# Edge-attribute gathers split between the sort and the ends of layers 1 and 2, and gate biases written to PSUM by ScalarE, in a four-layer graph network on one Trainium2 core

## The chip, the core and the metric

The kernel runs on one NeuronCore of a Trainium2 chip. The core has five instruction streams that run side by side: TensorE (PE, matmuls into the accumulator memory PSUM), VectorE (DVE), ScalarE (ACT), GpSimd (POOL) and SyncE (SP, which here only starts transfers). They wait for each other through semaphores. The metric is the device time of one execution in microseconds; lower is better.

## The reference

Four graph layers over 12,500 nodes (64 features) and 200,000 edges. After each one the nodes become `x = layernorm(x + layer(x))`. Cut to what matters:

```python
# layer 0: attention by destination, edge attributes of 2 columns, moments of z = x W_fc^T
a   = z[src] @ wa0 + z[dst] @ wa3 + e2_term + constant
out = segment_sum(softmax_by_dst(leaky(a))[:, None] * (z[src] + ez), dst)
# layer 1: plain sum
out = segment_sum(x[src], dst)
# layer 2: attention by source, edge attributes of 16 columns, then a gated update
h   = relu(concat(x[src], edge_attr_16, x[dst]) @ W_att1.T + b_att1)
alpha = softmax_by_src(h @ W_att2.T + b_att2)
msg = segment_sum(alpha[:, None] * (x[dst] @ W_lin.T + b_lin), src)
gi, gh = x @ W_ih.T + b_ih, msg @ W_hh.T + b_hh
r, z = sigmoid(gi_r + gh_r), sigmoid(gi_z + gh_z)
n   = tanh(gi_n + r * gh_n)
out = where(degree > 0, (1 - z) * n + z * msg, x)
# layer 3: attention by destination
out = segment_sum(softmax_by_dst(leaky(concat(x[src], x[dst]) @ W.T + b)) * x[src], dst)
```

(This text counts layers from 0, as the code does. The "ends of layers 1 and 2" of the short description are the ends of the first two, layers 0 and 1 here.)

## The kernel before

The program is a row of blocks. At the end of a block all five engines meet; the next block starts when the last of them is through.

**Block 1** sorts the edges by source. **Block 2** sorts them by destination (DVE, ACT and PE: a bitonic sort of 262,144 keys in 171 stages) and, beside that, brings the 16 attribute columns of each edge (with a one and the destination, 18 words, the array `rec16`) into source order. That is the work of `take_gpsimd`. The 200,704 places of an edge list are laid out as 128 partitions of W = 1568 columns, and one gather on POOL (`indirect_dma_start`) fetches one column, 128 rows of 72 bytes. `ESTEPS` = 196 steps of `G16` = 8 gathers fill a ring of 8 slots, `e_rows`; SP stores four steps at a time to `rec_s`. The steps are paced. While the sort runs, DVE also makes one-hot tables for a histogram, 200 steps, of which the first `BEGUN` = 24 are done in block 1. Step s of the gathers waits for histogram step `24 + s * 176 // ESTEPS` (line 733 makes it, the wait is in front of the gather of line 606). At three quarters of the steps POOL also sends 98 scatters (`scatter_seeds`, line 574).

**Blocks 3 to 6** are the four layers, made by `edge_layer`. In each POOL gathers 1568 columns of the node table (line 1202), and DVE and ACT form running sums along the sorted edges, which SP stores to `sums`. At the end of a layer comes a chain: the last sums are stored; POOL waits for that and gathers `ends` (line 1211); PE, DVE and ACT join the partial sums of the 128 partitions; SP stores `special` (line 1254); POOL waits for that and gathers the sums of the 98 node blocks, `got` (line 1218, 98 gathers). Seven groups of 14 node blocks are normed by DVE and ACT as they arrive (`normed_nodes`), and SP stores each to the next table (line 1755). At the end of layer 1 POOL, after `got`, scatters the new nodes (line 574, 98 scatters). Layer 2 then reads `rec_s`.

**The gated update** (`gated_nodes`) is the node stage of layer 2. Its 98 node blocks are cut into 28 parts, in each group of 14 three parts of four blocks and one of two. Each engine goes through a fixed order. At its step t, PE does `turn(t)` and `project(t-1)`. ACT does `own(t)`, `bend(t-3)`, `sigmoid_half(t-2)`, `keep(t-1)` and, where a part closes a group, `square`, `root` and `copy_rows`. DVE does `mix(t)`, `update(t-3)`, `candidate(t-2)` and, for closing parts, `center`, `variance` and `finish`. For one part: `turn` transposes (line 2044), `keep` copies that out of PSUM (line 1994), `project` adds the biases by three matmuls with a row of ones (line 2054, `bias4`) and then the products with `w_all` (line 2058), `sigmoid_half` (line 2002) reads the sums, `candidate`, `bend` and `update` (last line 1941) finish the part. `project(b)` may overwrite PSUM once `update(b-2)` is done (`new`). After `finish`, POOL scatters 14 columns of seeds for layer 3.

## Time and profile before

| | us |
|---|---|
| median of 3 runs | 11759.01 (11755.06 to 11760.62) |
| the profiled execution | 11769.89 |
| its span, first to last instruction | 11768.2 |
| busy: POOL | 8350.4 (71%) |
| busy: DVE | 5629.5 (48%) |
| busy: ACT | 2619.6 (22%) |
| busy: PE | 2530.8 (22%) |

The profile is of one execution. "Busy" is the time in which an engine worked on an instruction; time in which it waited, or in which its sequencer prepared the next one, is not counted. In the timeline a row gives the start, the duration, the engine, the line of the kernel, the operation and the tiles (written <- read), and in brackets how long the engine had been idle before and what ended that. "issue" means that it waited for nothing that is recorded. PEclk is the granted TensorE clock as a share of 2.4 GHz; its two levels are 0.5 and 1.0, and a stretch shows a mean of them.

### The profile page before, as it was taken

The numbers are of one execution on the slowest core, as the hardware profiler recorded it, in microseconds if no ns is written. First come the engines' busy times: TensorE is split into PE (matmuls) and PEld (weight loads), VectorE is DVE, ScalarE is ACT, GpSimd is POOL, SyncE is SP. The second block draws the span as 40 slices with busy tenths as digits, with TensorE's granted clock in tenths as the row PEclk, the third lists the DMA queues.
The fourth block names the chain that finished last, engine by engine and source line by source line (L and its number), as shares of the span: only waits on it lengthen the run. The fifth ranks groups of instructions, "written<-read, shape, count | busy, mean of one in ns | idle before, by whom it ended". The sixth has DMA issues, their size and how long they took to land. (4 is left out here: it accounts for less than half of the span.)

```text
span 11768.2 us, 56949 instructions
## 1 busy us (share of the span) xinstructions
PE 2530.8 (22%) x12070; PEld 2016.1 (17%) x12070; DVE 5629.5 (48%) x13769; ACT 2619.6 (22%) x3769; POOL 8350.4 (71%) x8546
## 2 busy tenths in 40 slices
PE   2322434320200000000000001666666640000000
PEld 2211323220200000000000000555555530000000
DVE  9999898970422222421111112677777542222223
ACT  1155555540111111112222220111111121111111
POOL 0077777777777777667777777777777657777776
PEclk8555555555555555555555555787888755555555
DMA  7000000011222222211111111333333212222222
GB/s 223 11 14 13 13 14 14 7 28 32 58 55 55 55 54 55 52 52 53 53 51 53 53 52 46 86 87 86 86 88 87 59 27 55 53 55 55 55 54 49
DMA packets 689050, 631.35 MB, mean 54 GB/s; under 512 B 453662, under 2 KB 511671, under 8 KB 687681
## 3 DMA queue, kind: packets, MB, share of 16 engines
q0 software_dynamic: 273056, 240.52, 10.7%
q1 hardware_dynamic: 414782, 380.90, 10.0%
q10 hardware_dynamic: 864, 6.29, 0.1%
q14 instruction: 252, 2.06, 0.1%
q8 instruction: 96, 1.57, 0.1%
HBM read 322.26 MB, written 304.83 MB: 53 GB/s over the span
## 5 line engine op out<-in xcount | busy, mean ns | idle before, releaser
L1202 POOL DMA_INDIRECT l_rows<-table,l_sources x4704 | 4477.1, 952 | 1474.8 <-issue 1433.4
L606 POOL DMA_INDIRECT e_rows<-in_rec,base x1568 | 1668.6, 1064 | 1059.8 <-DVE marks L733 579.0
L1202 POOL DMA_INDIRECT l_pair<-table,l_slab x1568 | 1505.1, 960 | 483.5 <-issue 459.6
L1401 DVE TENSOR_TENSOR_SCAN l_totals<-l_factor,banks 128x510 f32<-128x510 f32 (+3 forms) x672 | 752.8, 1162 | 1677.1 <-ACT banks L1556 1675.9
L1566 ACT COPY l_kept<-l_totals 128x476 f32<-128x476 f32 (+3 forms) x672 | 639.2, 967 | 3191.5 <-DVE l_totals L1401 3181.9
L1332 DVE TENSOR_TENSOR l_score<-l_rows,base 128x14 f32<-128x14 f32 x224 | 41.3, 185 | 2672.0 <-DMA l_rows<-table,l_sources 2672.0
L1518 PE MATMUL banks<-ident,l_kept 128*65 128x128 f32 (+2 forms) x4 | 1.9, 463 | 5865.0 <-DVE junk L1450 5865.0
L1518 PEld LDWEIGHTS banks<-ident,l_kept 128*65 128x65 f32 (+2 forms) x4 | 0.7, 170 | 5866.8 <-DVE junk L1450 5866.8
L751 PE MATMUL banks<-marks 125*128 125x98 bf16 x3200 | 623.3, 366 | 1235.3 <-DVE marks L733 1235.3
L388 DVE COPY_PREDICATED area<-banks,area 128x2048 f32<-128x2048 int32 x342 | 869.0, 2596 | 0.2
L751 PEld LDWEIGHTS banks<-marks 125*128 125x128 bf16 x3200 | 460.3, 148 | 1386.2 <-DVE marks L733 1282.0
L1508 PE MATMUL banks<-w_each,l_turned 128*128 128x288 f32 (+1 forms) x1344 | 658.7, 579 | 166.9 <-ACT l_turned L1588 166.9
L465 ACT COPY area<-area 128x2048 f32<-128x2048 f32 x342 | 642.8, 1930 | 0.2
L1320 DVE SCALAR_TENSOR_TENSOR l_junk<-banks,w_out 128x144 f32<-128x144 f32 x1568 | 407.9, 303 | 472.6 <-PE banks L1512 470.7
L1512 PEld LDWEIGHTS banks<-w_in,l_turned 128*128 128x128 f32 x3136 | 599.1, 235 | 190.0 <-issue 123.7
L1588 ACT COPY l_turned<-banks 128x512 f32<-128x512 f32 x448 | 248.1, 588 | 1673.1 <-PE banks L1497 1672.7
L1512 PE MATMUL banks<-w_in,l_turned 128*128 128x144 f32 x3136 | 606.8, 332 | 0.0
L1556 ACT COPY banks<-l_rows 128x476 f32<-128x476 f32 x224 | 196.0, 907 | 1504.4 <-DMA l_rows<-table,l_sources 1504.4
L462 ACT COPY area<-area 128x2048 f32<-128x2048 f32 x164 | 311.5, 1899 | 863.9 <-DVE area L388 800.9
L1425 DVE SCALAR_TENSOR_TENSOR l_kept<-l_kept,l_factor,l_message 128x65 f32<-128x65 f32 x1568 | 452.9, 289 | 81.2 <-DVE l_pair L1311 2.9
L382 DVE COPY_PREDICATED area<-banks,area 128x1024 f32<-128x1024 int32 x328 | 451.8, 1438 | 36.5 <-ACT area L462 32.4
L1497 PE MATMUL banks<-ident,l_pair 128*128 128x128 f32 x1568 | 270.8, 324 | 735.9 <-DMA l_pair<-table,l_slab 735.0
(310 smaller groups left out, 6302.7 us busy)
## 6 DMA issues: line engine op xcount, KB each, us to landing
l_rows<-table,l_sources POOLq DMA_INDIRECT x4704
sums<-l_kept SPq DMA_DIRECT2D x112, 476.0 KB
sums<-l_kept SPq DMA_DIRECT2D x224, 231.0 KB
sums<-l_kept SPq DMA_DIRECT2D x112, 462.0 KB
seeds<-zeros SPq DMA_DIRECT2D x130, 392.0 KB
sums<-l_kept SPq DMA_DIRECT2D x112, 448.0 KB
l_pair<-seeds SPq DMA_DIRECT2D x224, 224.0 KB, 3.3
e_rows<-in_rec,base POOLq DMA_INDIRECT x1568
```

The lines of the kernel that those rows point to most:

```text
L382: V.copy_predicated(key_to[:, :, i, :], swap.rearrange("p (x l) -> p x l", l=low), key_was[:, :, 1 - i, :])
L388: ins_ = V.copy_predicated(to[i], m, was[1 - i])
L465: AC.copy(to[i], was[i]).then_inc(s["copied"], 1)
L606: GP.indirect_dma_start(e_rows[:, u, g, :], None, A["rec16"], bass.IndirectOffsetOnAxis(e_ids[:, s * G16 + g:s * G16 + g + 1], 0)).then_in ...
L751: mm = PE.matmul(ps["ds".index(k)][:, 0:NB], hot[0][0:EP, i % HOTS, :, c], hot[1][0:EP, i % HOTS, 0:NB, c], start=s == 0 and c == 0, stop= ...
L1202: GP.indirect_dma_start(pair[:, u, g, 0:D] if gated else rows[:, u, g, :], None, table[l], bass.IndirectOffsetOnAxis(at, 0)).then_inc(rows ...
L1320: V.scalar_tensor_tensor(junk[:, g % 2, :], hidden_at(g), 0.0, extra["w_out"][:], ALU.max, ALU.mult, accum_out=score[:, u, g:g + 1]).then_ ...
L1401: V.tensor_tensor_scan(flat(totals[:, s % 2, h, 0:n, :]), flat(factor[:, s % 2, 0:n, :]), flat(fresh[s % 2][h][:, 0:n, :]), 0.0, ALU.mult, ...
L1425: V.scalar_tensor_tensor(kept[:, u, g, 0:M], old, factor[:, u, g:g + 1], message[:, u, g, :], ALU.mult, ALU.add).then_inc(kp.sem, 1)
L1508: PE.matmul(ps[4 + i][:, 0:n * H1], turned[:, u % 2, G * P:], extra["w_edge"][:, a:a + n, :].rearrange("p g h -> p (g h)"), start=True, st ...
L1512: mm = PE.matmul(hidden_at(g), turned[:, u % 2, g * P:(g + 1) * P], extra["w_in"][:], start=False, stop=True, skip_group_check=True)
L1566: AC.copy(kept[:, s % KR, :, a:a + n], totals[:, s % 2, h, 0:n, 1:G + 1].rearrange("p f g -> p g f")).then_inc(S["kept"].sem, 1)
```

## The change

It has two parts.

**Gathers.** `take_gpsimd` now stops 64 columns short: `ESTEPS` is (1568 - 64) / 8 = 188. The last 64 columns of attributes are fetched by POOL into a tile of their own, `late_rows`, in four pieces (`LATE_AT`): 22 behind the last node gather of layer 0 and ahead of the gather of `ends`, 14 at the very end of layer 0, 16 and 12 at the same two places of layer 1. SP fetches their ids in block 2 and stores `late_rows` to `rec_s` at the end of layer 1 (`save_late`). The tile of zeros of block 1 now lies in `late_rows`.

**Biases.** The three bias matmuls of `project` are gone. A tile `bias_all` holds the biases on all partitions (one matmul with ones and one copy at the start of layer 1, in place of three copies to `bias4`), and ACT copies it into the PSUM banks ahead of `keep`, in three copies (`set_bias`). `project(b)` waits for `biased(b)` in place of `new(b-2)`, and `set_bias(b)` waits for `new(b-2)`.

```diff
         G16 = 8
-        ESTEPS = W // G16
+        LATE_AT = ((0, 22), (22, 14), (36, 16), (52, 12))
+        LATE = sum(n for _, n in LATE_AT)
+        ESTEPS = (W - LATE) // G16
+        def take_late(pool, part):
+            a, n = LATE_AT[part]
+            pool.wait_ge(late_ids_in, 16)
+            for c in range(a, a + n):
+                GP.indirect_dma_start(late_rows[:, c, :], None, A["rec16"],
+                                      bass.IndirectOffsetOnAxis(late_ids[:, c:c + 1], 0)).then_inc(late_in, 16)
+        def save_late(sp):
+            sp.wait_ge(late_in, 16 * LATE)
+            sp.dma_start(rec_s.rearrange("(p c) w -> p c w", p=P)[:, W - LATE:, :], late_rows[:]).then_inc(late_saved, 16)
+            sp.wait_ge(late_saved, 16)
...
                     in_turn(STEPS, RING, [(0, one)])
+                    first_do.get("gpsimd_tail", nothing)(pool)
                     for u in range(KR):
                         pool.wait_ge(*saved[u].done(saves(u)))
...
                     then_do.get("gpsimd", nothing)(pool)
+                    first_do.get("gpsimd_end", nothing)(pool)
...
                     then_do.get("sync", nothing)(sp)
+                    first_do.get("sync_end", nothing)(sp)
...
             pe.wait_ge(w2_loaded, 16 * N_W2)
             PE.matmul(ps[6][:, 0:3 * D], w_lin[:], w_hh_t[:], start=True, stop=True)
             PE.matmul(ps[6][0:1, 3 * D:6 * D], b_col[:], w_hh_t[:], start=True, stop=True).then_inc(w2_mixed, 1)
+            pe.wait_ge(bias_made, 1)
+            PE.matmul(ps[7][:, 0:5 * D], ones[0:1, :], bias[:], start=True, stop=True).then_inc(bias_spread, 1)
...
+                    def set_bias(b, *_):
+                        g, v, a, n, o, u = of(b)
+                        if b >= 2:
+                            act.wait_ge(*new.done(b - 2))
+                        else:
+                            act.wait_ge(tail["kept"], 3)
+                        for to, at, w in sums_of(u):
+                            ins = AC.copy(to[:, 0:n, :], bias_all[:, None, at:at + w].to_broadcast([P, n, w]))
+                        ins.then_inc(biased.sem, 1)
...
-                    in_turn(N, 2, [(0, own), (3, bend), (2, sigmoid_half), (1, keep), (4, square), (5, root),
+                    in_turn(N, 2, [(0, own), (3, bend), (2, sigmoid_half), (1, set_bias), (1, keep), (4, square), (5, root),
                                    (6, copy_rows)])
...
                         pe.wait_ge(*kept.done(b))
-                        if b >= 2:
-                            pe.wait_ge(*new.done(b - 2))
-                        ways = ((both[u], 0, 2 * D), (hidden_in[u], 2 * D, 2 * D), (message_in[u], 4 * D, D))
-                        for to, at, w in ways:
-                            PE.matmul(to[:, 0:n, :].rearrange("p j f -> p (j f)"), ones[0:1, :],
-                                      bias4[:, J * at:J * at + n * w], start=True, stop=False, skip_group_check=True)
+                        pe.wait_ge(*biased.done(b))
                         for j in range(n):
-                            for to, at, w in ways:
+                            for to, at, w in sums_of(u):
```

How POOL's queue runs from block 2 to the end of layer 1, first before, then after the change (an `UNCONDITIONAL_BRANCH` is the edge of a block; lines 574 and 576 are the scatters, 606 and 625 the gathers of attributes, 1202 and 1223 those of nodes):

```order
L606 DMA e_rows<-in_rec,base 128x18 x392
L1053 UNCONDITIONAL_BRANCH
...
L1202 DMA l_rows<-table,l_sources 128x66 x1540
L1211 DMA l_ends<-sums,first_end_d 128x68
L1218 DMA got<-sums,end_at_d 128x68 x98
L1602 UNCONDITIONAL_BRANCH
...
L1202 DMA l_rows<-table,l_sources 128x64 x1568
L1211 DMA l_ends<-sums,first_end_d 128x64
L1218 DMA got<-sums,end_at_d 128x64 x98
L574 DMA seeds<-X,seed_at_s 213248x64 x98
```

```order
L625 DMA e_rows<-in_rec,base 128x18 x376
L1074 UNCONDITIONAL_BRANCH
...
L1223 DMA l_rows<-table,l_sources 128x66 x1540
L590 DMA late_rows<-in_rec,late_ids 128x18 x22
L1233 DMA l_ends<-sums,first_end_d 128x68
L1240 DMA got<-sums,end_at_d 128x68 x98
L590 DMA late_rows<-in_rec,late_ids 128x18 x14
...
L1223 DMA l_rows<-table,l_sources 128x64 x1568
L590 DMA late_rows<-in_rec,late_ids 128x18 x16
L1233 DMA l_ends<-sums,first_end_d 128x64
L1240 DMA got<-sums,end_at_d 128x64 x98
L576 DMA seeds<-X,seed_at_s 213248x64 x98
L590 DMA late_rows<-in_rec,late_ids 128x18 x12
```

The gathers of attributes ahead of the block's edge are 376 where they were 392 (and 1128 where they were 1176 ahead of the scatters), and four runs of late gathers stand on POOL at the ends of the two layers, two of them ahead of `ends`.

ACT in the gated update, around the second part of a group, before and after (line 1994, after it 2025, is `keep`; 2002, after it 2043, is `sigmoid_half`; 2034 is `set_bias`):

```order
L2007 ACTIVATE l_pair<-l_pair 128x128 [waits gru_reset]
L2002 ACTIVATE l_pair<-banks 128x512 [waits gru_new,gru_made]
L1994 COPY l_pair<-banks 128x512 [waits gru_made,gru_turned]
L1987 COPY l_pair<-X 128x2x64 [waits gru_turned]
L2007 ACTIVATE l_pair<-l_pair 128x256 [waits gru_reset]
```

```order
L2048 ACTIVATE l_pair<-l_pair 128x128 [waits gru_reset]
L2043 ACTIVATE l_pair<-banks 128x512 [waits gru_new,gru_made]
L2034 COPY banks<-bias_all 128x512 [waits gru_new]
L2034 COPY banks<-bias_all 128x512
L2034 COPY banks<-bias_all 128x256
L2025 COPY l_pair<-banks 128x512 [waits gru_made,gru_turned]
L2018 COPY l_pair<-X 128x2x64 [waits gru_turned]
L2048 ACTIVATE l_pair<-l_pair 128x256 [waits gru_reset]
```

`keep` now stands behind three copies, and behind their wait for `new`.

PE at the same place, before and after (2044 and 2085 are `turn`, 2058 and 2094 the products with `w_all`):

```order
L2044 MATMUL banks<-ident,l_pair 128x128 x3
L2054 MATMUL banks<-bias,ones 128x512 [waits gru_new,gru_kept]
L2054 MATMUL banks<-bias,ones 128x512
L2054 MATMUL banks<-bias,ones 128x256
L2058 MATMUL banks<-w_all,l_pair 128x128 x2
L2058 MATMUL banks<-w_all,l_pair 128x64
```

```order
L2085 MATMUL banks<-ident,l_pair 128x128 x3
L2094 MATMUL banks<-w_all,l_pair 128x128 [waits gru_biased,gru_kept]
L2094 MATMUL banks<-w_all,l_pair 128x128
L2094 MATMUL banks<-w_all,l_pair 128x64
L2094 MATMUL banks<-w_all,l_pair 128x128 x2
```

The three bias matmuls are gone from between `turn` and the products.

## Rows read from the trace of the kernel before

**Rows 1.** The page, part 1: busy time (share) and instructions of each engine.

```profile
PE 2530.8 (22%) x12070; PEld 2016.1 (17%) x12070; DVE 5629.5 (48%) x13769; ACT 2619.6 (22%) x3769; POOL 8350.4 (71%) x8546
```

**Rows 2.** Stretches of block 2: busy (instructions) of each engine, PEclk, DMA share, GB/s.

```profile
2600.00:2700.00 100.00, 0.00 (x0) 0.00 (x0) 0.00 (x0) 0.00 (x0) 75.66 (x80) 0.50 0.11 18
```

**Rows 3.** Stretches, line 606 alone: length, POOL busy (number of gathers), PEclk, DMA share, GB/s.

```profile
560.00:1201.00 641.00, 475.58 (x448) 0.50 0.09 13
...
2590.00:2880.00 290.00, 216.57 (x229) 0.50 0.13 26
```

**Rows 4.** Timeline: start, duration, engine, line, tiles, idle before; a paced gather; block 2's end.

```profile
1201.30 1.19 POOL L606 DMA_INDIRECT e_rows<-in_rec,base  x1 [2.25 <-DVE marks L733]
...
2875.26 0.95 POOL L606 DMA_INDIRECT e_rows<-in_rec,base  x1 [0.30 <-issue]
2884.35 0.32 SPq L1225 DMA_DIRECT2D l_sources<-dsrc  x1
```

**Rows 5.** Timeline, end of layer 0: POOL, DVE's last, SP's first of the next block.

```profile
4878.90 0.95 POOL L1202 DMA_INDIRECT l_rows<-table,l_sources  x1 [0.30 <-issue]
4895.77 0.97 POOL L1211 DMA_INDIRECT l_ends<-sums,first_end_d  x1 [15.93 <-DMA sums<-l_kept]
4905.26 0.95 POOL L1218 DMA_INDIRECT got<-sums,end_at_d  x1 [8.53 <-issue]
...
5026.61 0.94 POOL L1218 DMA_INDIRECT got<-sums,end_at_d  x1 [0.30 <-issue]
...
5042.98 1.09 DVE L1700 TENSOR_TENSOR X<-banks,l_var_n 128x896 f32<-128x896 f32 x1
5047.96 0.33 SPq L1225 DMA_DIRECT2D l_sources<-dsrc  x1
```

**Rows 6.** Timeline, end of layer 1: POOL, and the first instruction of layer 2's block.

```profile
7012.38 0.94 POOL L1202 DMA_INDIRECT l_rows<-table,l_sources  x1 [0.30 <-issue]
...
7023.34 0.94 POOL L1211 DMA_INDIRECT l_ends<-sums,first_end_d  x1 [10.02 <-DMA sums<-l_kept]
...
7280.45 0.97 POOL L574 DMA_INDIRECT seeds<-X,seed_at_s  x1 [0.30 <-issue]
7290.88 0.29 ACT L1581 COPY l_runs_on<-marks 128x7 f32<-128x7 f32 x2 [126.81 <-PEq L1602]
```

**Rows 7.** Groups of the gated update (9308 to 9635): busy, mean ns, idle before.

```profile
L2054 PE MATMUL banks<-bias,ones 1*128 1x512 f32 (+1 forms) x168 | 80.6, 624 | 14.4 <-ACT l_pair L1994 13.1 <-DVE l_pair L1941 1.1
```

**Rows 8.** Timeline of the gated update: a part of two blocks, and parts 12 and 13.

```profile
9391.94 1.35 PE L2054 MATMUL banks<-bias,ones 1*128 1x256 f32 x6 [0.51 <-ACT l_pair L1994]
...
9439.65 0.42 DVE L1941 SCALAR_TENSOR_TENSOR l_pair<-l_pair 128x256 f32<-128x256 f32 x1
...
9440.22 4.60 PE L2054 MATMUL banks<-bias,ones 1*128 1x512 f32 x6 [0.21 <-DVE l_pair L1941]
...
9444.75 5.38 PE L2058 MATMUL banks<-w_all,l_pair 128*128 128x128 f32 x24
...
9450.17 0.60 ACT L2002 ACTIVATE l_pair<-banks 128x512 f32<-128x512 f32 x1 [9.23 <-PE banks L2058]
9450.66 0.58 ACT L1994 COPY l_pair<-banks 128x512 f32<-128x512 f32 x1
...
9451.29 2.41 PE L2054 MATMUL banks<-bias,ones 1*128 1x512 f32 x6 [0.31 <-ACT l_pair L1994]
...
9453.64 4.47 PE L2058 MATMUL banks<-w_all,l_pair 128*128 128x128 f32 x24
```

**Rows 9.** Groups of layer 1, two kinds of ACT copy: busy, mean ns, idle before.

```profile
L1556 ACT COPY banks<-l_rows 128x476 f32<-128x476 f32 x112 | 107.3, 958 | 1504.4 <-DMA l_rows<-table,l_sources 1504.4
...
L1549 ACT COPY l_factor<-marks 128x476 f32<-128x476 f32 x112 | 65.6, 586 | 26.6 <-DVE junk L1268 26.6
```

**Rows 10.** Stretches of the gated update: busy (instructions) of each engine, PEclk, DMA share, GB/s.

```profile
9395.00:9434.00 39.00, 31.22 (x122) 23.57 (x122) 21.33 (x42) 11.24 (x23) 29.86 (x31) 0.65 0.22 38
...
9545.00:9606.00 61.00, 32.70 (x118) 24.86 (x118) 39.30 (x66) 15.97 (x28) 27.50 (x27) 0.57 0.09 16
```

More of the change, by code:

```diff
@@ L176, in build @@
         padded = sem("padded")
+        late_ids = sbt(top, "late_ids", [P, 64], I32)
+        late_rows = sbt(top, "late_rows", [P, 64, RE])
+        zeros = late_rows[:].rearrange("p c w -> p (c w)")[:, 0:W // 2]
         layer0 = ExitStack()
@@ L612, in take_sync @@
         def take_sync(sp):
-            sp.dma_start(e_ids, sid[0:NQ].rearrange("(p c) -> p c", p=P)).then_inc(e_ids_in, 16)
+            ids = sid[0:NQ].rearrange("(p c) -> p c", p=P)
+            sp.dma_start(e_ids, ids).then_inc(e_ids_in, 16)
+            sp.dma_start(late_ids[:], ids[:, W - LATE:]).then_inc(late_ids_in, 16)
             to = rec_s.rearrange("(p c) w -> p c w", p=P)
@@ L1804, in build @@
         bias = sbt(gated_ctx, "bias", [1, 5 * D])
-        bias4 = sbt(gated_ctx, "bias4", [1, 4 * 5 * D])
+        bias_all = sbt(gated_ctx, "bias_all", [P, 5 * D])
         w3 = sbt(gated_ctx, "w3", [P, 2, D])
@@ L1809, in build @@
         w2_made = Chain(sem("w2_made"))
+        bias_made, bias_spread = sem("bias_made"), sem("bias_spread")
         N_W2 = 29
@@ L1849, in gated_weights_vector @@
             link(V.tensor_copy(bias[:, 3 * D:4 * D], b_row[:, 2 * D:3 * D]))
-            link(V.tensor_copy(bias[:, 4 * D:], b_row[:, 6 * D:]))
-            for a, n in ((0, 2 * D), (2 * D, 2 * D), (4 * D, D)):
-                link(V.tensor_copy(bias4[:, 4 * a:4 * (a + n)].rearrange("p (j f) -> p j f", j=4),
-                                   bias[:, None, a:a + n].to_broadcast([1, 4, n])))
+            V.tensor_copy(bias[:, 4 * D:], b_row[:, 6 * D:]).then_inc(bias_made, 1)
+            dve.wait_ge(bias_spread, 1)
+            link(V.tensor_copy(bias_all[:], ps[7][:, 0:5 * D]))
         layer_ctx = ExitStack()
@@ L1887, in stage @@
                 of_group = lambda n: again(f"gru_{n}", 1, len(groups))
-                mixed, owned, turned, kept, made, gated, reset, tanh, new = (
-                    of_part(n) for n in ("mixed", "owned", "turned", "kept", "made", "gated", "reset", "tanh", "new"))
+                mixed, owned, turned, kept, made, gated, reset, tanh, new, biased = (
+                    of_part(n) for n in ("mixed", "owned", "turned", "kept", "made", "gated", "reset", "tanh", "new",
+                                         "biased"))
+                sums_of = lambda u: ((both[u], 0, 2 * D), (hidden_in[u], 2 * D, 2 * D), (message_in[u], 4 * D, D))
                 centered, squared, spread, rooted, x_done, near_done, copied = (
```

13 lines of the change are left out of this document (8 added, 5 removed).

## The prediction

> **What bounds the kernel now.** I read the page first: POOL is busy 71% of the span, no other engine over half [rows 1]. Since the blocks follow each other, each place that the change touches has its own last engine, so I read the timeline at four places.
>
> *Block 2.* From 2600 on PE, DVE and ACT do nothing, and POOL gathers attributes alone, 80 in 100 us [rows 2]. In the last stretch 229 gathers take from 2590 to 2876.2, which is 1.25 us each (0.95 busy, 0.30 between) [rows 3, 4]. The next block begins 8.1 us after the last gather's end. POOL ends this block by far, so a gather less is 1.25 us less, unless it is paced.
>
> *Ends of layers 0 and 1.* In layer 0 POOL is idle for 15.9 us between its last node gather and `ends`, and 8.5 us more until `got`; after its last `got` (end 5027.6) DVE still works to 5044.1, and the next block starts at 5048.0 [rows 5]. In layer 1 the first pause is 10.0 us. But its last engine is POOL: the last scatter ends at 7281.4, and the next block starts 9.5 us later [rows 6]. The reader should see that three of the four places are pauses with a length, and the fourth is none.
>
> *The gated update.* The bias matmuls take 80.6 us in all [rows 7], and they follow `keep` and precede the products, on the chain by which one part ends: `sigmoid_half`, `keep` of the next part, biases, products, `sigmoid_half` again [rows 8]. What POOL does there (98 scatters) ends last, but its last 14 wait for DVE's last group, so the chain sets the end.
>
> **The change, part by part.** The sum is made against the profiled execution (11769.9 us, of which 11768.2 is the span). It is 10.9 us above the median of the runs; I take that off at the end.
>
> *Block 2: -60.* Without pacing 64 gathers x 1.25 would be 80 us. But the first steps are paced by DVE. The last wait of some length is at 1201.30, after 448 gathers, at step 56 [rows 3, 4]; it asks for histogram step 24 + 56*176//196 = 74. After the change each step asks for a later one: histogram step 74 is asked for by step 54 (54*176//188 = 50). The table comes at the same time, so at 1201 POOL has 54 steps behind it and not 56. Left are 188 - 54 = 134 steps where 140 were. DVE's part of the block is untouched, so the 6 steps are missing at the end, where POOL is alone: 6 x 8 x 1.25 = 60 us. Past 1201 no pacing is near: 1120 gathers in 1675 us include 98 scatters, some 11 us a step, and the histogram needs less. Bounds: 50 (POOL loses another step to the pacing) and 80 (none at all).
>
> *22 gathers ahead of `ends` in layer 0: +11.9.* The 23rd slot after the gather at 4878.90 starts at 4878.90 + 23 x 1.25 = 4907.7, where `ends` now starts at 4895.8 [rows 5]. All that comes after `ends` shifts with it, the second pause too, which is a wait for the chain that `ends` starts. Of 27.5 us of gathers 15.6 are covered.
>
> *14 at the end of layer 0: +6.6.* The last one would end at 5027.55 + 17.5 = 5045.1. The block does not end there: at the end of layer 1 9.5 us lie between POOL's last transfer and the next block [rows 6], in block 2 8.1 [rows 4]. With 9.5 the next block starts at 5054.6, not at 5048.0 [rows 5]. With 8.1 it is 5.2.
>
> *16 in layer 1's tail: +10.3.* 7012.38 + 17 x 1.25 = 7033.6 against 7023.3 [rows 6].
>
> *12 at the end of layer 1: +15.0.* POOL is last there, so all 12 are paid. SP's store of `late_rows` starts when the last has landed and lies inside the same 9.5 us; if it takes longer than they last, up to 3 us come on top.
>
> So 36 of the 80 us are covered, 43.8 are paid, and the gathers give -60.0 + 43.8 = **-16.2**.
>
> *The gated update: -27.* The three copies are priced by two rows. An ACT copy of 476 columns between SBUF tiles, with a repeated operand, takes 0.586 us; one that writes PSUM, with a strided read, 0.958 [rows 9]. `sigmoid_half` and `keep`, 512 columns each, start 0.49 apart [rows 8]. By the first row three copies (512, 512, 256 columns) are 1.4 us for a part of four blocks and 0.9 for one of two; by the second 2.4. I take 1.4: the read of `bias_all` runs along contiguous columns, as in the first row.
>
> The biases cost 4.6 or 2.41 us by the clock for four blocks, 1.35 for two [rows 8]. Step by step:
> - Part 0: `set_bias` is done before there is data. -4.6.
> - Part 4, same chain, low clock: 4.6 - 1.4 = 3.2.
> - 14 parts, second and third of each group. Out of 80.6 us seven first parts take 7 x 4.6 and seven short ones 10.8, so these have 37.6, 2.7 each: 37.6 - 14 x 1.4 = 18.0.
> - Parts 8 to 24, every fourth: before them DVE does `finish`, then `update(b-2)` (ends 9440.07), then the biases start (9440.22) [rows 8]. Now `set_bias` waits for that update and `keep` stands behind it: 1.4 + 0.6 in place of 4.6. The short part's `set_bias` also stands ahead of `root`, for which `finish` waits, 1.0. Each 1.6, five times 8.0.
> - Parts 3 and 27: 2.1 together. The other short parts are behind `finish`: 0.
>
> Sum 35.9. Against it stands the clock. The products take 5.38 us at the lower and 4.47 at the higher level [rows 8]. PE is busy 31.2 of 39 us with a mean clock of 0.65, and in the last stretch 32.7 of 61 with 0.57 [rows 10]. Without the biases PE is busy some 20 of 35, as in the second row, so I price all products at the lower level: eight parts with 0.9 more and three with 0.5, 8.7. That leaves **-27**. Bounds: -6 (copies at 2.4 us: 21 more) and -38. The Trainium skill (TensorE: Matmul & The Clock Gate, Part 1) says that the clock follows how busy PE has been of late, a rule that speaks against taking matmuls away; by it the stage gives 27, without it 36. The Trainium skill (ScalarE: Activation LUTs, ACT is a hardware spline evaluator) calls PSUM ScalarE's faster destination; the PSUM row of this trace is the slower of the two, but its read is strided too. By the page the destination adds nothing and 1.4 and 27 stand; by the row taken as it is they are 2.4 and 6.
>
> *At nothing:* the extra matmul and copy of `bias_all` at the start of layer 1 (about 1 us more on DVE, while the first rows are still on their way), and the load of the 64 ids.
>
> Sum: 11769.9 - 60.0 + 43.8 - 27 = 11726.7 for the profiled execution, less 10.9: **11716 us** against the median of 11759 (-0.37%).
>
> **The rivals.**
> *A. No change that can be measured.* ACT's copies cost as the PSUM row says, and the stage gives 6. With 16 of the gathers that is -22: 11737. For it: the one row that writes PSUM. Against it: its read pattern, also seen in slow copies.
> *B. The clock stays up.* PE's work shrinks, but so do its waits. The stage gives 36 to 38: 11706.
> *C. Pacing costs nothing* (POOL makes up its lost steps, since it has fewer to do while DVE disturbs it): -80 in block 2, 11696. Against it: 1201.30 is a wait for DVE.
> *D. Slower.* `keep` and with it every product stands behind `set_bias`. If the copies into PSUM are held while PE writes there, ACT becomes the chain. The stage breaks even at 1.4 + 27/21 = 2.7 us a part, the kernel at 1.4 + 43/21 = 3.4, and it is 0.2% slower from 1.4 + 66.5/21 = 4.6, where a copy takes three times the 0.586 row. At 5 us it is 11716 + 21 x 3.6 = 11792. Against it: nothing in the trace shows an ACT copy beyond 1.0 us at that size.
>
> **How the numbers follow.** Forecast 0.62, A 0.16, B 0.12, C 0.06, D 0.04. The likeliest gives 11716. The range reaches from 11699 (between B and C) to 11741 (A; with block 2 at its bound of 50 it would be 11747) and leaves out about 2 in 10. A measurement of this kernel can tell 0.2%, 23.5 us, from no change. Faster by more: forecast, B and C, 0.80; within: A, 0.16; slower: 0.04.
>
> **What would show it.** In the new profile: block 2's last attribute gather at about 2815; the step that waits for the histogram near 1201 with 432 gathers behind it; `ends` of layer 0 12 us later after the last node gather than before, with no wait for the saves; a gap of 8 to 9.5 us between POOL's last transfer and the start of layers 1 and 2; `set_bias` copies of 0.6, 0.6 and 0.35 us; products of 5.4 us at PEclk 0.5; and the stage from the first `keep` to the last scatter some 27 us shorter. Wrong would be: a new wait between ACT and DVE at each part, late gathers of more than 1.25 us each, or a block 2 shorter by 80.

## The result, and the profile after

The changed kernel takes **11700.35 us** (median of 5 runs, 11698.78 to 11708.72), the kernel before 11759.01 (5 runs beside them, 11753.46 to 11762.34). The ratio is 0.9954, with a 95% interval of 0.9942 to 0.9966: 58.7 us or 0.5% faster. The forecast was 11716 (11699 to 11741). Sign and range hold; the middle is 16 us too high, and nearly all of that is one term.

The profiled execution of the changed kernel took 11700.35 us, its own median, with a span of 11698.6. The one of before was 10.9 us above its median, so differences between the two profiles hold some 11 us that belong to neither part of the change.

Busy times first (part 1 of the page after; engine, busy us, share of the span, instructions). They answer to [rows 1]: POOL is as busy as before, PE is 96 us less busy, ACT 32 more.

```profile
PE 2434.3 (21%) x11904; PEld 1961.6 (17%) x11904; DVE 5630.7 (48%) x13767; ACT 2651.5 (23%) x3853; POOL 8344.7 (71%) x8546
```

The timeline after, POOL and SP at the places of [rows 4] (start, duration, engine, line, operation and tiles, idle time before and its releaser):

```profile
1200.98 1.68 POOL L625 DMA_INDIRECT e_rows<-in_rec,base  x1 [3.01 <-DVE marks L754]
...
2814.19 0.94 POOL L625 DMA_INDIRECT e_rows<-in_rec,base  x1 [0.30 <-issue]
...
2823.28 0.32 SPq L1248 DMA_DIRECT2D l_sources<-dsrc  x1
...
2827.97 0.94 POOL L1223 DMA_INDIRECT l_rows<-table,l_sources  x1 [12.84 <-DMA l_sources<-dsrc]
...
4814.40 0.94 POOL L1223 DMA_INDIRECT l_rows<-table,l_sources  x1 [0.30 <-issue]
4815.65 0.94 POOL L590 DMA_INDIRECT late_rows<-in_rec,late_ids  x1 [0.30 <-issue]
...
4843.16 0.94 POOL L1233 DMA_INDIRECT l_ends<-sums,first_end_d  x1 [0.30 <-issue]
4852.49 0.94 POOL L1240 DMA_INDIRECT got<-sums,end_at_d  x1 [8.39 <-DMA sums<-l_special]
...
4973.58 0.94 POOL L1240 DMA_INDIRECT got<-sums,end_at_d  x1 [0.30 <-issue]
4974.82 0.94 POOL L590 DMA_INDIRECT late_rows<-in_rec,late_ids  x1 [0.30 <-issue]
...
4991.05 0.94 POOL L590 DMA_INDIRECT late_rows<-in_rec,late_ids  x1 [0.30 <-issue]
...
5001.52 0.33 SPq L1248 DMA_DIRECT2D l_sources<-dsrc  x1
...
6962.15 0.95 POOL L1223 DMA_INDIRECT l_rows<-table,l_sources  x1 [0.30 <-issue]
6963.41 0.94 POOL L590 DMA_INDIRECT late_rows<-in_rec,late_ids  x1 [0.30 <-issue]
...
6983.38 0.94 POOL L1233 DMA_INDIRECT l_ends<-sums,first_end_d  x1 [0.30 <-issue]
...
7252.30 0.94 POOL L590 DMA_INDIRECT late_rows<-in_rec,late_ids  x1 [0.30 <-issue]
...
7254.81 0.33 SPq L595 DMA_DIRECT2D rec_s<-late_rows  x1
...
7263.24 0.94 POOL L1210 DMA_INDIRECT l_first<-table,node_s  x1 [10.00 <-POOLq L1626]
```

Read it against [rows 4 to 6]. The wait near 1201 us is still there, with 432 gathers behind it. The last attribute gather starts at 2814.19. `ends` of layer 0 follows the last late gather without a wait. SP's store of the late rows, issued at 7254.81, lies inside the gap that follows POOL's last transfer.

| term | before | after | change | forecast |
|---|---|---|---|---|
| first gather of layer 0 | 2888.93 | 2827.97 | -61.0 | -60.0 |
| layer 0, end of the last node gather to `ends` | 15.9 | 27.8 | +11.9 | +11.9 |
| layer 0, last `got` to the first gather of layer 1 | 25.1 | 31.7 | +6.6 | +6.6 |
| layer 1, end of the last node gather to `ends` | 10.0 | 20.3 | +10.3 | +10.3 |
| layer 1, last scatter to the next block | 10.5 | 25.0 | +14.6 | +15.0 |
| gated update, first `got` gather to the last scatter | 314.9 | 275.2 | **-39.8** | **-27** |
| sum | | | -57.4 | -43.2 |

The sum of -57.4 lies close to the 58.7 us between the medians. The two spans differ by 69.6 us. The 12.2 us that are left between them lie in the loops of the layers (3.5, 3.8 and 3.8 us shorter in layers 0, 1 and 3, 1.4 longer in layer 2) and in the `got` stage of layer 1 (2.7 shorter), which the change does not touch. The profile of before stood 10.9 us above its median, so that is about where its surplus would be; no second trace of either kernel on this machine shows it.

Now the stage that gave more. ACT and PE in one group of 14 blocks, after, in the timeline (for [rows 8]):

```profile
9392.94 5.38 PE L2094 MATMUL banks<-w_all,l_pair 128*128 128x128 f32 x24 [2.08 <-ACT l_pair L2025]
...
9400.83 2.89 PE L2094 MATMUL banks<-w_all,l_pair 128*128 128x128 f32 x24 [1.65 <-ACT l_pair L2025]
...
9424.58 1.41 ACT L2034 COPY banks<-bias_all 128x512 f32<-128x512 f32 x3 [5.70 <-DVE l_pair L1972]
9425.93 0.58 ACT L2025 COPY l_pair<-banks 128x512 f32<-128x512 f32 x1
...
9426.56 4.56 PE L2094 MATMUL banks<-w_all,l_pair 128*128 128x128 f32 x24 [2.08 <-ACT l_pair L2025]
...
9431.16 0.60 ACT L2043 ACTIVATE l_pair<-banks 128x512 f32<-128x512 f32 x1 [3.30 <-PE banks L2094]
9431.65 1.41 ACT L2034 COPY banks<-bias_all 128x512 f32<-128x512 f32 x3
```

The three copies of `set_bias` take 1.41 us for four blocks. `keep` and the products follow in the order that was forecast, and the new wait for `update` stands ahead of `set_bias` (5.70 us). But products of four blocks also take 2.89 us. The granted clock in three such products, and below it that of four groups, after (window, length, busy time and instructions of PE, PEld, DVE, ACT, POOL, PEclk, DMA share, GB/s):

```profile
9392.94:9398.32 5.38, 5.38 (x25) 5.38 (x26) 0.87 (x3) 1.30 (x3) 4.16 (x5) 0.50 0.81 113
9400.82:9403.71 2.89, 2.88 (x24) 2.75 (x24) 2.75 (x5) 0.47 (x2) 2.28 (x3) 1.00 0.15 26
9433.62:9438.07 4.45, 4.45 (x26) 4.43 (x26) 4.28 (x8) 0.46 (x2) 3.54 (x4) 0.63 0.02 0
...
9356.60:9488.50 131.90, 72.47 (x392) 67.15 (x392) 83.64 (x166) 62.88 (x132) 100.58 (x98) 0.69 0.19 26
```

And the same of before, for the two products that the forecast took as the two levels, and for four groups:

```profile
9444.75:9450.13 5.38, 5.38 (x26) 5.38 (x26) 0.00 (x0) 0.00 (x0) 4.16 (x5) 0.50 0.04 5
9453.64:9458.11 4.47, 4.47 (x27) 4.47 (x26) 3.96 (x8) 0.00 (x0) 3.34 (x4) 0.62 0.02 0
...
9399.90:9550.10 150.20, 120.50 (x488) 91.17 (x488) 83.96 (x165) 43.45 (x84) 85.86 (x85) 0.66 0.11 20
```

Products wholly at 1.2 GHz take 5.38 us, wholly at 2.4 GHz 2.89. The 4.47 us of before were a mixture (clock 0.62), not the higher level. Over four groups PE's share of work fell from 80% to 55%, and the clock did not fall with it (0.66 and 0.69). A group takes 33.0 us (a quarter of 131.9) after 37.6 (of 150.2).

### The profile page after: what moved, and what is told of

It is laid out like the page before. It is cut to its first block and busy times, and to the rows that moved or that the text cites. A ratio compares the mean times of both kernels' runs of the same rounds, so it can differ in the third digit from the quotient of the medians.

```text
span 11698.6 us, 56700 instructions
## 1 busy us (share of the span) xinstructions
PE 2434.3 (21%) x11904; PEld 1961.6 (17%) x11904; DVE 5630.7 (48%) x13767; ACT 2651.5 (23%) x3853; POOL 8344.7 (71%) x8546
## 5 line engine op out<-in xcount | busy, mean ns | idle before, releaser
L625 POOL DMA_INDIRECT e_rows<-in_rec,base x1504 | 1611.0, 1071 | 1056.1 <-DVE marks L754 605.1
L1356 DVE TENSOR_TENSOR l_score<-l_rows,base 128x14 f32<-128x14 f32 x224 | 43.4, 194 | 2662.8 <-DMA l_rows<-table,l_sources 2662.8
L1403 DVE TENSOR_TENSOR banks<-l_rows,banks 128x476 f32<-128x476 f32 x448 | 423.9, 990 | 5.9 <-ACT banks L1565 5.9
```

Of the source, the lines that this page charges most:

```text
L625: GP.indirect_dma_start(e_rows[:, u, g, :], None, A["rec16"], bass.IndirectOffsetOnAxis(e_ids[:, s * G16 + g:s * G16 + g + 1], 0)).then_in ...
L1403: V.tensor_tensor(fresh[s % 2][h][:, 0:n, 1:G + 1], rows[:, u, :, a:a + n].rearrange("p g f -> p f g"), w.to_broadcast([P, n, G]), ALU.mul ...
```

## The experiments

The experiments ran on three other chips than the comparison above. There the kernel before takes 13338 to 13379 us, not 11759. The median gather of nodes is as long as in the first traces (0.94 us), and so are the copies and matmuls; but the late gathers of `z_after` take 1.08 us, and the node gathers of layer 0 start 1.45 us apart on average (`z_before`) where it was 1.27. `x_gathers`, `x_biases`, `x_pace` and `x_warm` ran on one chip, `y_pace`, `y_full`, `x_nobias` and `x_tight` on the second, `z_before`, `z_after`, `x_nopace` and `x_cover` on the third. So each run is read against the kernel before that ran beside it, and against `z_before`. An experiment of these shows what a part does there; it does not measure again the sizes of the first comparison.

**1. The gathers alone** (`x_gathers`), the three bias matmuls and `bias4` put back:

```diff
-                        pe.wait_ge(*biased.done(b))
+                        if b >= 2:
+                            pe.wait_ge(*new.done(b - 2))
+                        for to, at, w in sums_of(u):
+                            PE.matmul(to[:, 0:n, :].rearrange("p j f -> p (j f)"), ones[0:1, :],
+                                      bias4[:, J * at:J * at + n * w], start=True, stop=False, skip_group_check=True)
```

> The gathers alone: the 64 late gathers as in the changed kernel, the biases by matmuls as before. If the two parts of the change don't touch each other, block 2 ends 60 us earlier, the four pieces add 11.9, 6.6, 10.3 and 15, and the kernel is 16 us faster than before (ratio 0.9986); the stage of the gated update stays at 315 us (first `got` gather to the last scatter). Rival: the loops of the layers, which were 3.5 to 3.8 us shorter in three of the four layers of the changed kernel's profile, are shorter because of the late gathers; then they are shorter here too, against this kernel's own time, and it gains some 28 us (0.9976).

Measured: 1.0035 (1.0015 to 1.0055), slower by 35 us of the medians, where -16 was expected.

**2. The biases alone** (`x_biases`), with `ESTEPS = W // G16` and no late gathers:

> The biases alone: `set_bias` on ScalarE as in the changed kernel, all 196 steps of attribute gathers in block 2. From the two traces the stage of the gated update should take 275 us, 40 less than before, and the kernel should be 40 us faster (0.9966). The forecast, which let the products fall to the lower clock, had 27 less (0.9977). If the 40 came partly from the gathers, the stage is longer than 275 here.

Measured: 0.9983 (0.9960 to 1.0006), the stage 401.9 us, with 417.5 in `x_gathers` and 410.8 in `z_before`. The direction holds, the size does not, on this machine. The 1568 node gathers of layer 0 take 2278 us in `x_gathers` and 2279 here, those of layer 1 2175 and 2169, so the late gathers don't make the loops shorter; that rival falls.

**3. Both kernels there** (`z_before`, one execution, and `z_after`), unchanged:

> The kernel before, unchanged, once with a profile. The experiments so far ran on machines on which the kernel before takes 13338 to 13379 us, not 11759, and their traces show POOL's gathers, DVE's copies and ACT's copies as long as ever, but stretches in which engines wait for nothing that is recorded. This run gives the trace to compare with. Expected: block 2 ends with DVE's sort, not with POOL's gathers; the gathers of layers 0, 1 and 3 start 1.38 us apart, not 1.25; the stage of the gated update takes 417 us, as in x_gathers, not 315.

> The changed kernel, unchanged, on such a machine. If its two parts add up there as measured alone (x_gathers +35 us, x_biases -16), it is 19 us slower than before (1.0014). On a machine as in the first comparison it is 0.9954. Rival: the parts help each other there too, and it is faster than before (below 0.998).

Measured: in `z_before` the node gathers start 1.45, 1.38 and 1.38 us apart on average in layers 0, 1 and 3, and the stage of the gated update takes 410.8 us. `z_after` takes 0.9994 (0.9971 to 1.0016). The ratios of the parts measured alone add up to 1.0018, just outside that interval; with the intervals of the two parts, some 0.002 each, this does not speak against their adding up. So the change that gains 0.5% in the first comparison gains nothing that can be measured here.

From trace to trace: the four pieces cost 15.6, 14.7, 12.7 and 19.1 us, together 62.1 where 43.4 were paid at first, because the late gathers start some 1.4 us apart, not 1.25, and the block's end lasts longer.

And the four places are not all: from the first gather of layer 0 to the first of layer 2 `z_after` takes 5002 us and `z_before` 4925, 77 more, as in `x_gathers` against `x_biases` (76). Of the 15 us beyond the four places some 6 lie in the loop of layer 1 and 6 in its `got`; why was not looked into.

The stage of the gated update gives 7.2 us, not 39.8, and `x_gathers`, with the same stage as `z_before`, took 6.7 longer in it than that kernel, so 7.2 is known to a few us only. Of the 128 us that the stage of `z_after` is longer than in the first comparison, 112 are two waits of ACT at its beginning (59.4 and 52.5) for the semaphore that PE sets behind the products.

Block 2 is ended by DVE's sort there. The first instruction behind the sort (line 686 before, 707 after), in the timelines of `z_before` and then of `z_after`:

```profile
3123.43 1.98 DVE L686 TENSOR_SCALAR area<-area 128x2048 int32<-128x2048 int32 x1
```

```profile
3045.00 1.98 DVE L707 TENSOR_SCALAR area<-area 128x2048 int32<-128x2048 int32 x1
```

POOL's last attribute gathers end at 3041.5 and 2969.4, so 82 and 76 us ahead of it. Of the sort's 78 us no more than a part is the change's: the five runs with its gathers and its pace have this instruction at 3103, 3078, 3049, 3045 and 3031.

**4. The pace** (`x_pace`, and the same kernel again on another machine as `y_pace`):

```diff
-                paced = BEGUN + s * (2 * HSTEPS - BEGUN) // ESTEPS
+                paced = BEGUN + s * (2 * HSTEPS - BEGUN) // (W // G16)
```

> The changed kernel with one number changed: the pace of the attribute gathers is worked out with 196 steps again, so step s waits for the same histogram step as in the kernel before. If the pacing cost two of the eight steps, POOL has 448 gathers behind it at the wait near 1201 us (432 in the changed kernel), and layer 0 begins 20 us earlier: block 2 is 80 us shorter than before, the kernel 20 us faster than the changed one (0.9937 of before). Rival: the missing steps were lost to something else (memory traffic or the sort beside it), the wait near 1201 is no limit, and the start of layer 0 moves by less than 5 us.

> The same kernel as x_pace: the changed kernel, with the pace of the attribute gathers worked out with 196 steps again. There the machine handed out instructions late on all engines (13338 us for the kernel before), DVE's sort ended block 2 at 3115 and the pace could not matter. If this run is on a machine on which the kernel before takes some 11760 us again, the expectation is the first one: 448 gathers behind POOL at the wait near 1201 us, layer 0 begins 20 us earlier than in the changed kernel (2808 in place of 2828), and the kernel takes 11680 (0.9933 of before). Rival: the start of layer 0 moves by less than 5 us, 11700.

Measured: 1.0044 (1.0022 to 1.0067) and 1.0065 (1.0040 to 1.0090). Where 20 us less were expected it is slower than the changed kernel (0.9994, on another chip), by more than the intervals. On one and the same chip `y_pace` stands clear of `y_full` (1.0013, up to 1.0028), which has the changed kernel's pace, while `x_pace` does not stand clear of `x_gathers` (1.0035) and `x_warm` (1.0013, up to 1.0037). The instruction behind the sort comes at 3104 and 3161 us, against 3031 to 3103 with the changed kernel's pace. Whether the two steps come back where POOL ends the block was not measured. But the pace does something that my forecast did not see, so I took it away altogether.

**5. No pace** (`x_nopace`), the two lines with the wait for the histogram taken out:

> The changed kernel with the wait for the histogram taken out of the attribute gathers, so POOL runs ahead of DVE's sort as fast as it can. With the pace loosened by 4% (x_pace, y_pace) the kernel was 1.0044 and 1.0065 of before, where kernels with the same gathers and the changed kernel's pace (x_warm, y_full) were 1.0013. If gathers that run early delay the sort, this is worse still: over 1.007. If the pace does not matter where the sort ends block 2, it is 1.001. On a machine as in the first comparison, where POOL ends block 2, it should gain the 43 us that POOL waits there: 0.992.

Measured: **1.0800** (1.0772 to 1.0829), over 1000 us slower. In `x_nopace` POOL gathers without a pause until 2091 us. Windows before and behind that point (columns as above):

```profile
600.00:2090.00 1490.00, 178.57 (x535) 76.15 (x536) 427.01 (x322) 236.73 (x129) 1158.10 (x1082) 0.50 0.11 14
2100.00:2600.00 500.00, 175.74 (x912) 138.46 (x912) 447.44 (x298) 244.78 (x160) 0.00 (x0) 0.53 0.00 0
```

What DVE waits for in the first of them, and then the DMA queues of it (packets, MB, share of 16 engines):

```profile
DVE marks L752 <- remote: 940.1, 30, 34.7
DVE marks L752 <- issue: 103.7, 3, 34.7
```

```profile
q0 software_dynamic: 34622, 10.04, 9.2%
q1 hardware_dynamic: 4896, 10.03, 1.7%
q8 instruction: 4, 0.07, 0.0%
q14 instruction: 12, 0.10, 0.0%
```

While POOL gathers DVE works 427 of 1490 us, and when POOL stops 447 of 500. "remote" is what the profile writes when it finds no instruction that ended a wait. The kernel says what line 752 waits for: it may overwrite a one-hot table once PE has counted an earlier one (`summed`, set behind the matmuls of line 770). The same wait in the first comparison is put down to PE:

```profile
DVE marks L754 <- PE banks L772: 6.4, 10, 0.7
```

So PE has to be looked at. Its matmuls of one histogram step, first in the first comparison, then in `x_nopace` around one of DVE's waits, and what PE waits for there between 600 and 2090 us:

```profile
1286.34 3.15 PE L772 MATMUL banks<-marks 125*128 125x98 bf16 x16 [12.79 <-DVE marks L754]
```

```profile
1123.14 0.14 PEld L770 LDWEIGHTS banks<-marks 125*128 125x128 bf16 x1 [2.65 <-issue]
1124.13 1.10 POOL L623 DMA_INDIRECT e_rows<-in_rec,base  x1 [0.30 <-issue]
1124.54 0.34 PE L770 MATMUL banks<-marks 125*128 125x98 bf16 x1 [2.46 <-issue]
1125.53 1.09 POOL L623 DMA_INDIRECT e_rows<-in_rec,base  x1 [0.30 <-issue]
1125.94 0.14 PEld L770 LDWEIGHTS banks<-marks 125*128 125x128 bf16 x1 [2.66 <-issue]
1125.95 1.23 DVE L752 TENSOR_TENSOR marks<-count_j,work 125x2048 bf16<-125x2048 bf16 x1 [34.69 <-remote]
```

```profile
PE banks L770 <- issue: 1294.9, 526, 3.2
```

In the first comparison 16 matmuls of a step take 3.15 us. Here PE gets out one instruction, a weight load or a matmul, every 1.40 us, and a step of 16 of each takes 44.8 us, which is the distance from one of DVE's long waits to the next. So DVE waits for PE, and PE waits for nothing recorded. PE is back at 16 matmuls in 3.15 us at 2122.84, some 30 us after POOL's last gather. `z_after` has such stretches too, but short ones (up to 1332 us, for one, with matmuls mostly 2.8 us apart).

The two queues named "instruction" move 16 packets in 1490 us; in the same window of `z_after`, where POOL pauses for the pace, they move 35, and DVE works 1185 us. That count alone decides nothing, since engines that get less done also need fewer instructions. The reading: PE's instructions come late while POOL gathers without a pause, so the pace is what keeps the sort going. The rows show that the two go together; that the gathers hold up PE's instructions, and by what way, is inferred and not shown. The expectation of `y_pace` spoke of late instructions on all engines; the rows here show them on PE. The Trainium skill (Runtime: NRT & Kernel Launch, Instruction fetch mechanics) says that each sequencer fetches through a DMA queue of its own and that the cost is mostly hidden. If fetching is what PE's waits are, it was not hidden on these machines; in the first comparison there are no such waits (41 packets in the same window, and DVE waits in it only for ACT and PE, 8.5 us at most).

**6. A tighter pace** (`x_tight`):

```diff
-                paced = BEGUN + s * (2 * HSTEPS - BEGUN) // ESTEPS
+                paced = min(2 * HSTEPS - 1, BEGUN + s * (2 * HSTEPS - BEGUN) // (ESTEPS - 8))
```

> The changed kernel with the pace of the attribute gathers tightened: the divisor is 180 in place of 188 (196 in x_pace). Theory, from x_nopace (while POOL gathers without a pause DVE works 28% of the time and 89% once it stops): the other engines get their instructions in POOL's pauses, so more pauses end the sort earlier. In the changed kernel's run on such a machine POOL's last attribute gather was at 2969 and DVE's sort ended at 3055, so there is room; divisor 196 cost 0.3% to 0.5%, so 180 should give about as much: the sort ends 40 to 60 us earlier, the kernel is at 0.995 to 0.997 of before. Rival: the pace matters only where it is taken away altogether, and x_pace was a chance; then 0.999 to 1.002. On a machine as in the first comparison, where the gathers end the block, the tighter pace costs one or two steps more, 10 to 20 us.

Measured: **0.9967** (0.9951 to 0.9982), the size that the theory gave. The instruction behind the sort, in `x_tight`'s timeline:

```profile
3001.89 1.98 DVE L707 TENSOR_SCALAR area<-area 128x2048 int32<-128x2048 int32 x1
```

It comes earlier than in each of the five runs with the changed kernel's pace, and in `x_nopace` it comes at 4052. It is the one version that is faster than before on these machines by more than its interval. Its interval ends below that of `y_full` on the same chip (0.9997 to 1.0028) but overlaps those of `z_after` and `x_nobias`, so that the tighter pace beats the changed kernel's is likely and not settled. Nor is it shown that it works by way of PE's late instructions.

**7. Fewer late columns** (`x_cover`):

```diff
-        LATE_AT = ((0, 22), (22, 14), (36, 16), (52, 12))
+        LATE_AT = ((0, 12), (12, 8), (20, 8), (28, 4))
```

> The changed kernel with 32 late columns in place of 64, in pieces that the pauses of the first comparison cover: 12 and 8 in layer 0, 8 and 4 in layer 1. On a machine as in the first comparison: three of the eight steps that 32 columns are (four, less one for the pace) leave block 2, -30 us, and some 7 us are paid (4 x 1.25 for the last piece, 1 or 2 for the rest); with the biases' -40 that is 11759 - 63 = 11696, the changed kernel's time within 5 us, with half the columns moved. Where block 2 ends with the sort, nothing is gained in it; half of the 61 us that the four pieces cost there (x_gathers against x_biases) are paid: between x_biases (0.9983) and the changed kernel (1.0014).

Measured: 0.9984 (0.9965 to 1.0003), not to be told from `z_after` beside it. But in the traces the pieces cost 2.2, 9.0, 2.5 and 6.6 us against `z_before`: 20.3 us for 32 columns where 64 cost 62.1. The pieces inside the pauses ahead of `ends` are nearly free at their own place, as the forecast priced them. From the first gather of layer 0 to the first of layer 2, though, `x_cover` takes 4956 us, 32 more than `z_before`, where 64 columns take 77 more; 5 of the 11 us beyond the four places lie in the `got` of layer 1.

**8. Work added on TensorE** (`x_warm`, `y_full`), one more matmul behind each part's products and four behind a group's last:

```diff
                         mm.then_inc(made.sem, 1)
+                        for _ in range(4 if b in closes else 1):
+                            PE.matmul(ps[6 + u][:, 0:512], ones[0:1, :], bias_all[0:1, None, 0:128].to_broadcast([1, 4, 128]),
+                                      start=True, stop=True, skip_group_check=True)
```

In `y_full` the added call is `PE.matmul(ps[6 + u][:, 0:5 * D], ident[:], w_all[:], ...)`.

> The changed kernel with work added on TensorE: after the products of a part it writes a transposing bank that no one needs at that time, with one matmul of 512 columns, after the last part of a group with four. Its results are not used. In the forecast the clock followed TensorE's share of work; if so the products of four blocks, 2.9 to 5.4 us in the changed kernel, mostly 4.5, now take 2.9 nearly always, the granted clock of the stage rises from 0.66 to 0.71 to over 0.9, and a group of 14 blocks takes some 6 us less (33.1 to 27), until the scatters on POOL end last: its 98 take at least 98 x 1.29 = 127 us after `got`, so the stage can shrink by 13 to 20 us. Rival: the clock does not follow, the added matmuls (up to 1.9 us each at the lower level) delay the turns and the products, and the stage is up to 10 us longer.

> The changed kernel with work added on TensorE as in x_warm, but each added matmul uses all 128 rows and columns of the array (identity x the 320 columns of w_all) and not one row. In x_warm PE was busy 28 of 38 us and the granted clock was 0.63, no higher than without (18 of 38 us, 0.63 to 0.69), and the bias matmuls of before, one row each, gave 31 of 38 us and 0.60 to 0.64. First theory: what one row does counts for nothing towards the clock, what 128 rows do counts; then the clock rises here to over 0.85, the products of four blocks take 2.9 us most of the time (4.5 now), a group of 14 blocks takes some 5 us less, and the stage 13 to 20 us less until POOL's scatters end last. Second theory: the clock of this stage has nothing to do with how much is added; it stays at 0.6 to 0.7 and the stage is 0 to 10 us longer.

Measured: `x_warm` 1.0013 (0.9990 to 1.0037), `y_full` 1.0013 (0.9997 to 1.0028). Four groups in `z_before`, `z_after`, `x_warm` and `y_full`, one row each (columns as above, PEclk third from the end):

```profile
10775.20:10926.10 150.90, 123.82 (x488) 94.31 (x488) 83.87 (x166) 43.78 (x84) 56.95 (x56) 0.64 0.08 13
```

```profile
10762.10:10912.60 150.50, 74.71 (x392) 69.33 (x392) 83.94 (x166) 62.46 (x132) 57.55 (x56) 0.68 0.07 13
```

```profile
10799.40:10950.60 151.20, 111.56 (x452) 82.31 (x450) 83.75 (x166) 62.41 (x132) 56.54 (x56) 0.65 0.08 13
```

```profile
10790.90:10941.70 150.80, 84.46 (x448) 72.32 (x448) 83.79 (x165) 62.44 (x132) 56.16 (x56) 0.77 0.07 13
```

Matmuls of one row take PE's busy time from 75 to 112 us, and the clock stays where it was (0.68, 0.65). Matmuls of 128 rows take it to 84 only, and the clock is 0.77. The products of the 21 parts of four blocks take together 105.0 us in `z_before`, 100.9 in `z_after`, 102.6 in `x_warm` and 91.5 in `y_full`; in eight runs with the biases on ACT and nothing added (the changed kernel at first, `z_after`, `x_biases`, `x_pace`, `y_pace`, `x_nopace`, `x_cover`, `x_tight`) they take 95.7 to 104.4, in three with bias matmuls (the kernel before at first, `z_before`, `x_gathers`) 104.6 to 105.5. So taking the bias matmuls away did not lengthen the products: their sum did not rise in any of the eight. What raised the clock in `y_full` is less certain. It is one trace, and in `x_nobias` (below), where nothing is added, the products also take only 90.7 us, at a clock of 0.68 over four groups. The Trainium skill (TensorE: Matmul & The Clock Gate, Part 1) says the clock follows how busy PE has been; with busy time as the profile counts it, the four rows above don't follow that.

The stage did not get shorter in `y_full` (403.1 us after 403.6), though its products did. In each group ACT waits once, in `z_after` as in `y_full`, ahead of `sigmoid_half` of the second part; here from `z_after`:

```profile
10820.32 0.60 ACT L2043 ACTIVATE l_pair<-banks 128x512 f32<-128x512 f32 x1 [8.49 <-remote]
```

The wait is for the semaphore that PE sets behind the products (`made`). The last of them ends at 10816.76 by the records (the profile models the ends of matmuls), and the semaphore moves at 10820.30, 3.5 us later. In the first comparison it moves within 0.1 us of that end. In four groups of `y_full` it moves 4.5 to 6.1 us after it, so what the products gain there is lost in this gap. What fills the gap is not recorded.

**9. No biases** (`x_nobias`), `set_bias` and its wait taken out and `start=True` in the products:

> The changed kernel with set_bias left out and no biases added in the gated update (they are left out of the result; the products alone start each accumulation). It prices ScalarE's copies. On a machine as in the first comparison each group of 14 blocks has three copies of 1.41 us and one of 0.87 on its chain, so the group falls from 33.1 to some 28 us until POOL's scatters end last, and the kernel is 13 to 20 us faster than the changed one. On machines as in the experiments a group takes 37.3 to 37.8 us whether the biases are on ScalarE (z_after) or on TensorE (z_before), and once in each group ScalarE waits some 8.5 us for nothing recorded ahead of the second part's sigmoid_half. Theory: that wait, not the copies, sets the group; then it stays at 37 us or more here too, and the kernel is within 10 us of the changed one. Rival: the copies are on the chain there too, and a group falls to 33 us or less.

Measured: 0.9996 (0.9976 to 1.0016), so the medians can't tell it. In the trace a group takes 33.2 us on average (35.6 to 36.0 and 29.4 to 29.7 in turn), not 37.6, and the stage 373.9 us, 29.7 less than in `z_after`. The rival's first half is right, the copies are on the chain there too; its 33 us or less holds in every second group. But 29.7 is not the price of the copies. Every second group keeps a long wait, now 11.2 us, and is 1.6 to 2.0 us shorter than in `z_after`; in the others the wait is short (5.3 us) and the group is 8 us shorter, which is more than the 5.1 us of copies in it. Of these 5.1 us, 3.5 come back against a group of the first comparison, in which no such wait fell (29.6 after 33.1). Why every second group here has a short wait only was not looked into.

## Why the prediction was right, and where it was not

- **Block 2, -60: right.** 61.0. The two lost steps are in the trace: 432 gathers behind the wait near 1201 us, where before 448 were. That they were lost to the pace and to nothing else rests on these rows; `x_pace` was to show it and ran where the sort ends the block. Rival C, 80 us, falls.
- **The pacing was taken for a loss only.** The forecast priced the wait as 20 us given away. The runs showed that on other machines the sort goes on only with it (`x_nopace` 1.08; in small steps `x_pace` 1.0044, `y_pace` 1.0065, `x_tight` 0.9967). In the first comparison the traces have no such waits, so the sum was not wrong by it.
- **The four pieces: right to 0.5 us** (11.9, 6.6, 10.3, 14.6 against 11.9, 6.6, 10.3, 15.0). The gap behind POOL's last transfer was what decided two of them, and 9.5 us was the right one of the two rows. On the other machines the same pieces cost 62.1 us at these places, and layers 0 and 1 together are 77 us longer.
- **`set_bias`: right.** 1.41 us and 0.87 for 1.4 and 0.9. Rival A (2.4 us a part) and D (copies held while PE writes) fall: the longest of the 84 copies took 0.593 us. `x_nobias` shows the copies on the chain, as the sum had them, though not their whole price.
- **The clock, 8.7 us taken off: wrong, and the step that made the middle too high.** The stage gave 12.8 us more than forecast, of the 16 that the kernel did. The step was "without the biases PE is busy some 20 of 35, so I price all products at the lower level". PE's share fell as said (72 of 132 us), but the products took 95.7 us in sum after 104.6, where the forecast had them 8.7 longer. Two things were wrong in it: 4.47 us was read as the higher level when the clock in that row is 0.62, so how much a product could gain (2.89) was not seen; and the bias matmuls were counted as work that holds the clock up, which the clock does not bear out: 0.66 with them and 0.69 without, and 0.65 in `x_warm`, where as much work of the same kind was added again. Without that term the forecast is -36 for the stage and 11707 for the kernel. The measured -39.8 is rival B's 36 to 38 and 2 more. B's way, a clock that stays up, is what happened, but the sum is not confirmed term by term: 35.9 and the 8.9 us that the products became shorter would be 44.8, some 5 more than measured, and which of the terms was too high was not taken apart.
- **The profile's 10.9 us above the median: it fits.** The six terms give 57.4, the medians 58.7, and 12.2 us between the two profiles lie outside the six.
- **Not foreseen: the machine.** Rows of one trace can't show that elsewhere DVE's sort ends block 2, or that PE's instructions and its semaphore come late for no recorded reason, so that ACT waits 8.5 us in each group. There the same change is at 0.9994, so the gain of 0.5% is shown for the machine of the first comparison only.

## What to carry to other kernels

Price moved transfers by the length of the pause they go into, and put there no more than it holds: at their own places 32 columns cost 20 us where 64 cost 62. Then check the price over the whole stretch, where it was 32 and 77. Before a clock term goes into a sum, read the granted clock inside the very instructions that are to change; two durations of one operation need not be the two levels. A wait that paces a DMA stream may be there for the engines beside it: take it away alone once, before its cost is booked as a gain. And where the profile names no releaser of a wait, look up in the kernel which semaphore it is and look at the engine that sets it.

## What was not expected of the hardware

- With gathers back to back on POOL, PE got out one weight load or matmul every 1.40 us in `x_nopace` and waited for nothing recorded, and DVE, which waits for its counts up to 34.7 us at a time, worked 29% of the time (427 of 1490 us); 89% once the gathers stopped.
- One kernel took 11759 us in one place and 13338 to 13379 in others, with the median node gather at the same 0.94 us; much of what differs is time in which an engine waits for nothing recorded.
- With matmuls of one row added (37 us more in 151) the granted clock was 0.65 after 0.68, and with 10 us of matmuls of 128 rows it was 0.77, each in one trace.
- Between POOL's last transfer and its first of the next block, at the end of layer 1, lie 10.5 and 10.0 us in the first comparison, 16.8 (`z_before`) and 19.1 (`z_after`) in the experiments.
- In `z_after` the semaphore behind PE's products moved 3.5 us after the recorded end of the last one in the second part of a group, within 0.1 us in the first comparison.
